# Layer 1 of a graph network: TensorE sums source rows and edge attributes by node column, with the one-hot's node numbers read from PSUM

## The chip, the cores and the metric

The kernel runs on 1 core of one Trainium2 chip. The time is device microseconds (us) of one launch. Engines are written as in the profile: PE (TensorE), DVE (VectorE), ACT (ScalarE), POOL (GpSimd), SP (SyncE, which here only issues DMAs).

## The reference, cut to what matters

There are 12,500 nodes of 128 features and 200,000 edges, sorted by target `dst`. Two layers follow each other, each with a residual and a layer norm.

```
# layer 0: attention over edges and self loops
xl, xr = x @ W_l, x @ W_r
e      = sum(leaky_relu(xl[src] + xr[dst], 0.2) * att)      # 4 heads
p      = softmax of e over the edges of a target
y      = layernorm(segment_sum(p * xl[src], dst) + bias + x) * gamma + beta
x      = layernorm(x + y)
# layer 1: message passing and a two-layer MLP
neigh  = segment_sum(x[src] + edge_attr, dst)
h      = (2 * x + neigh) @ W1 + b1
h      = where(h > 0, h, 0.01 * h)
x      = layernorm(x + h @ W2 + b2)
```

Everything is float32.

## The kernel before, in words

Edges are cut into 196 groups of 1,024 (`G`): 128 partitions by 8 edges (`T`). Nodes are padded to 100 blocks of 128. The program has five stages with a barrier of all engines between two of them (`end_phase`):

1. Linear products of all nodes. The table `xl_table` (132 columns: 128 features and 4 linear attention terms) is written to HBM.
2. Layer 0's edges: for each group POOL gathers 1,024 rows of `xl_table` by 8 indirect DMAs (line 469), PE, ACT and DVE compute the softmax and the sums.
3. Self loops, merge and the two layer norms; `x1_table` (128 columns) is written to HBM. POOL clears `xr`, which then holds `neigh`.
4. Layer 1's edges, the stage that the change rewrites.
5. The MLP and the last layer norm, over 50 pairs of blocks.

**Stage 4.** SP runs through the groups in `load_group` (line 448): once the group's ring slot is free (`rows_free1`, one of 4 slots, `U`), it loads the 1,024 source numbers (`src_idx`, line 454), then, once `dst_taken1` allows it, the targets (`dst_near`, line 458) and the attributes (512 KB into `dst_row`, line 1053). POOL waits for the source numbers and issues 8 indirect DMAs of 128 rows (`gather`, line 469). DVE, in order, for each group: subtracts the first node of the target's block from the targets (`dst_rel`, line 1105); makes a one-hot of 128 x 8 x 128 by comparing `dst_rel` with the numbers 0 to 127 in `node_row` (line 1109), both in SBUF; waits for the gather and the attributes; adds the two into `relu_h` (line 1125); frees the slot; and then adds the sum that PE made of the group before into `neigh` (line 1113). PE multiplies one-hot by message, 8 products of 128 x 128 x 128, each two instructions (line 1075). Where a group's targets lie in a second block (or more), DVE makes one more one-hot and PE sums once more (`further_visits`), and both wait for each other. One visit's one-hot therefore comes with one PE sum and one addition.

The loops over groups are `sweep`: a head, a loop of 4 groups a round, and a tail, with the ends of each group's targets loaded into registers. In stage 4 these ends are block numbers (`bounds`); in stage 2 they are the first node and the number of further windows of 128 nodes that start at that first node (`spans`).

**Stage 5.** `node_loop` interleaves steps of neighbouring pairs on each engine. For a pair: SP loads x1; DVE makes h = 2 x1 + neigh (line 1233); PE transposes it (line 1175); ACT copies it to SBUF (line 1205); PE multiplies with W1 (line 1183); ACT adds b1 (line 1210); DVE applies the slope (line 1238); PE adds residual, b2 and the product with W2 (lines 1192 to 1195); DVE takes the statistics; ACT takes the root, scales (line 885) and issues the store (line 1219).

## Time and profile before

| | |
|---|---|
| three runs | 4748.25, 4744.81, 4747.33 us; median 4747.33 |
| the profiled execution, its own time | 4730.89 us |
| its span (first to last instruction) | 4729.0 us |
| busy PE, DVE, ACT, POOL | 68%, 54%, 13%, 70% of the span |
| mean granted TensorE clock | 0.836 |
| HBM traffic | 464.45 MB read, 47.30 MB written, mean 108 GB/s |
| stages, start of each (us) | 0, 114, 2292, 2495, 4601 |

Busy shares are averages over stages with different limits, so the stage that is changed is read by itself. An instruction that only issues a DMA, waits, or works on registers is not counted as busy; an indirect DMA on POOL is, since POOL makes its descriptors.

### The profile page before, as it was taken

The numbers are of one execution on the slowest core, as the hardware profiler recorded it, in microseconds if no ns is written. First come the engines' busy times: TensorE is split into PE (matmuls) and PEld (weight loads), VectorE is DVE, ScalarE is ACT, GpSimd is POOL, SyncE is SP. The second block draws the span as 40 slices with busy tenths as digits, with TensorE's granted clock in tenths as the row PEclk, the third lists the DMA queues.
The fourth block names the chain that finished last, engine by engine and source line by source line (L and its number), as shares of the span: only waits on it lengthen the run. The fifth ranks groups of instructions, "written<-read, shape, count | busy, mean of one in ns | idle before, by whom it ended". The sixth has DMA issues, their size and how long they took to land. (4 is left out here: it accounts for less than half of the span.)

```text
span 4729.0 us, 71029 instructions
## 1 busy us (share of the span) xinstructions
PE 3216.0 (68%) x16994; PEld 2342.8 (50%) x16995; DVE 2549.1 (54%) x7518; ACT 592.0 (13%) x1636; POOL 3300.4 (70%) x3295
## 2 busy tenths in 40 slices
PE   6899999999999999999593433343333434433448
PEld 4555555565555655555483333343333333333337
DVE  7577677667666666766483333333333333333337
ACT  3111111111111111111260000000000000000006
POOL 3777777777777777776246777777777777777750
PEclk9899999999999999999796667766766676677669
DMA  6544444444444444443443333333333333333323
GB/s 183 164 111 112 112 113 112 112 112 113 113 112 113 112 112 113 112 113 99 110 114 99 103 99 95 104 100 99 104 96 102 99 100 99 99 104 99 98 71 100
DMA packets 463435, 512.49 MB, mean 108 GB/s; under 512 B 183038, under 2 KB 363134, under 8 KB 463398
## 3 DMA queue, kind: packets, MB, share of 16 engines
q1 hardware_dynamic: 280646, 262.38, 19.2%
q0 software_dynamic: 100352, 208.93, 18.0%
q10 hardware_dynamic: 82400, 40.77, 3.0%
q8 instruction: 13, 0.21, 0.0%
q14 instruction: 24, 0.20, 0.0%
HBM read 464.45 MB, written 47.30 MB: 108 GB/s over the span
## 5 line engine op out<-in xcount | busy, mean ns | idle before, releaser
L469 POOL DMA_INDIRECT rows<-xl_table,src_idx x1568 | 1587.9, 1013 | 533.6 <-issue 513.2
L469 POOL DMA_INDIRECT rows<-x_table,src_idx x1568 | 1598.6, 1020 | 489.4 <-issue 476.8
L1075 PE MATMUL pT<-relu_h,node_of 128*128 128x128 f32 x1584 | 367.8, 426 | 1017.8 <-DVE node_of L1109 1017.8
L1075 PEld LDWEIGHTS pT<-relu_h,node_of 128*128 128x128 f32 x1584 | 341.2, 327 | 1039.0 <-DVE node_of L1109 1039.0
L535 PE MATMUL ph<-node_of,xr_win 128*128 128x512 f32 x784 | 752.7, 1094 | 1.3 <-issue 1.3
L1075 PE MATMUL pA<-relu_h,edge_of 128*128 128x128 f32 x3136 | 483.7, 319 | 259.7 <-DVE relu_h L1125 259.7
L1075 PEld LDWEIGHTS pA<-relu_h,edge_of 128*128 128x128 f32 x3136 | 461.9, 234 | 278.9 <-DVE relu_h L1125 278.9
L1125 DVE TENSOR_TENSOR relu_h<-rows,dst_row 128x1024 f32<-128x1024 f32 x196 | 241.0, 1229 | 566.0 <-DMA rows<-x_table,src_idx 566.0
L572 PE MATMUL pA<-wmsg,edge_of 128*128 128x136 f32 x3168 | 425.7, 288 | 6.8 <-DVE edge_of L789 6.3
L561 PE MATMUL pT<-att_heads,relu_h 128*128 128x56 f32 x3136 | 391.3, 278 | 1.3 <-DVE shifted L818 1.3
L572 PEld LDWEIGHTS pA<-wmsg,edge_of 128*128 128x128 f32 x3168 | 385.6, 192 | 11.4 <-issue 8.0
L647 ACT ACTIVATE relu_h<-ph 128x512 f32<-128x512 f32 x392 | 234.2, 597 | 1187.7 <-PE ph L535 1177.2
L561 PEld LDWEIGHTS pT<-att_heads,relu_h 128*128 128x128 f32 x3136 | 365.9, 192 | 28.2 <-DVE shifted L818 1.4
L535 PEld LDWEIGHTS ph<-node_of,xr_win 128*128 128x128 f32 x784 | 154.1, 218 | 272.8 <-issue 272.4
L1205 ACT ACTIVATE node_of<-ph 128x256 f32<-128x256 f32 x50 | 19.2, 384 | 2146.2 <-PE ph L1175 2121.8
L1109 DVE TENSOR_TENSOR edge_of<-dst_rel,node_row 128x1024 f32<-128x1024 f32 x196 | 240.2, 1226 | 24.1
L526 PE MATMUL ph<-ident,rows 128*128 128x128 f32 x1568 | 238.2, 302 | 13.9 <-DMA rows<-xl_table,src_idx 13.9
L789 DVE TENSOR_TENSOR edge_of<-dst_rel,node_row 128x1024 f32<-128x1024 f32 x198 | 244.0, 1232 | 6.8
L1113 DVE TENSOR_TENSOR xr<-xr,pT 128x128 f32 x99 | 28.5, 288 | 400.2 <-PE pT L1075 400.2
L763 DVE TENSOR_TENSOR wmsg<-rows,wmsg 128x1024 f32<-128x1024 f32 x196 | 239.1, 1220 | 4.8 <-ACT r_exp L682 4.8
L1105 DVE TENSOR_SCALAR dst_rel<-dst_near,block_base 128x8 f32<-128x8 int32 x295 | 73.3, 248 | 270.7 <-DVE xr L1113 162.0
L526 PEld LDWEIGHTS ph<-ident,rows 128*128 128x128 f32 x1568 | 194.7, 155 | 38.4 <-issue 26.3
(154 smaller groups left out, 3637.6 us busy)
## 6 DMA issues: line engine op xcount, KB each, us to landing
dst_row<-in_dst SPq DMA_DIRECT2D x196, 513.0 KB
dst_row<-in_edge_attr SPq DMA_DIRECT2D x195, 512.0 KB
rows<-xl_table,src_idx POOLq DMA_INDIRECT x1568
rows<-x_table,src_idx POOLq DMA_INDIRECT x1568
sums_table<-win ACTq DMA_DIRECT2D x198, 68.0 KB
rows<-in_x SPq DMA_DIRECT2D x100, 128.0 KB, 2.4
xr_win<-xr_table SPq DMA_DIRECT2D x196, 64.0 KB
sums_table<-win ACTq DMA_DIRECT2D x1, 6868.0 KB
```

What stands on the lines that cost most here:

```text
L469: pool.indirect_dma_start(rows[s][:, t, 0:table.shape[1]], None, table[:, :], bass.IndirectOffsetOnAxis(ap=src_idx[s][:, t:t + 1], axis=0))\
L526: pe.matmul(h[:, t, :], rows[s][:, t, 0:D], ident[:, :], start=(t % 4 == 0), stop=False, is_transpose=True)
L535: return [pe.matmul(h[:, k:k + 4, :], xr_of[:, :], by_tile[:, k:k + 4, :], start=False, stop=stop) for k in range(0, T, 4)]
L561: pe.matmul(out_t[:, t, :], relu_h[0][:, t, :], att_heads[:, :], start=(t == 0), stop=False)
L572: ins = pe.matmul(pA[k][:, 0:WC], edge_of[k][:, t, :], w[:, t, :], start=(t == 0), stop=(t == T - 1 and k == 1))
L647: act.activation(relu_h[0][:, k:k + 4, :], h, ACT.Relu, scale=1.0 - GAT_SLOPE)\
L763: v.tensor_tensor(heads[:, :, :, 0:C], rows[s][:, :, 0:D].rearrange("p t (h c) -> p t h c", h=H), heads[:, :, :, C:HC].to_broadcast([P, T, ...
L789: one_hot = lambda k: v.tensor_tensor(edge_of[k][:, :, :], dst_rel[:, :].unsqueeze(2).to_broadcast([P, T, P]), node_row[:, :].unsqueeze(1) ...
L1075: ins = pe.matmul(banks[k][:, 0:D], edge_buf[k][:, t, :], m[:, t, :], start=(t == 0), stop=(t == T - 1))
L1105: v.tensor_scalar(dst_rel[:, :], dst_near[g.c % U][:, 1:T + 1], block_base[:, bass.ds(blk(b), 1)], None, ALU.subtract).then_inc(S("visit1_ ...
L1109: return v.tensor_tensor(edge_buf[k][:, :, :], dst_rel[:, :].unsqueeze(2).to_broadcast([P, T, P]), node_row[:, :].unsqueeze(1).to_broadcas ...
L1125: v.tensor_tensor(msg[g.c % 2][:, :, :], rows[s][:, :, 0:D], attr[s][:, :, :], ALU.add)\
```

## The change

- Stage 1 also computes `firsts`: each group's first target in every partition (a row of 196 numbers spread by a product with ones).
- Stage 4 loads all groups' targets with one DMA at its start (`dst_all`, 196 x 8 numbers in each of 128 partitions) and DVE subtracts `firsts` once (`rel_all`). The load of each group's targets falls away.
- The one-hot counts from the group's first target (as in stage 2), not from the block's first node. Its second input, the numbers 0 to 127, is in PSUM (`row_bank`).
- DVE's addition of rows and attributes falls away: PE sums both, attributes first and rows after, into one bank: 16 products in place of 8. Data are the stationary operand and the one-hot the moving one, so the sum comes out transposed: `neigh_t` has features in partitions and nodes in columns, and a window may start at any column.
- Four banks and four one-hots, one for each slot; DVE adds a bank three groups later (`LAG`). Slots are freed by PE's `neigh_summed`, not by DVE.
- Further windows are worked off by both engines before the main one of their group.
- Stage 5: PE transposes x1 itself, DVE adds `neigh_t` to twice that from PSUM and writes the transposed h, and ACT's copy falls away.

```diff
@@ sweep: head, body and tail shifted by back (LAG in stage 4)
-    part("head", None, 0, [0], 0, 2)
+    part("head", None, 0, range(back), 0, max(2, back))
     with eng.Fori(0, groups // U - 1) as j:
-        part("body", j, 0, range(1, U + 1), 0, U + 2)
+        part("body", j, 0, range(back, U + back), 0, U + max(2, back))
@@ stage 1
+                pe.wait_ge(S("first_ready"), 1)
+                pe.matmul(firsts_bank, ones[:, :], first_f[:, :], start=True, stop=True).then_inc(S("first_spread"), 1)
...
+                v.wait_ge(S("first_spread"), 1)
+                v.tensor_copy(firsts[:, :], firsts_bank)
@@ stage 4
+        banks = [t[:, 0:P] for t in (pA[0], pA[1], pT1, pT2)]
+        more_bank, row_bank = ph[0][:, 0, :], ph[1][:, 0, :]
             @block.sync
             def _(sp):
+                sp.dma_start(dst_all, bass.AP(a["dst"].tensor, 1, [[T, P], [G, groups], [1, T]])).then_inc(S("dsts_in"), 16)
+
+                def load(g, parts=P):
+                    s = g.c % U
+                    sp.wait_ge(S("neigh_summed"), g.times(1, 1))
+                    sp.dma_start(src_idx[s][:, :], bass.AP(a["src"].tensor, g.times(G), [[T, P], [1, T]]))\
+                      .then_inc(S(f"src_in1{s}"), 16)
                     src = bass.AP(a["edge_attr"].tensor, g.times(G * D), [[T * D, parts], [1, T * D]])
+                    sp.dma_start(attr[s][0:parts].rearrange("p t d -> p (t d)"), src).then_inc(S(f"attr_in{s}"), 16)
...
             @block.tensor
-                def visit(k, m):
-                    for t in range(T):
-                        ins = pe.matmul(banks[k][:, 0:D], edge_buf[k][:, t, :], m[:, t, :],
-                                        start=(t == 0), stop=(t == T - 1))
+                def visit(bank, s, one_hot):
+
+                    for k, m in enumerate((attr[s], rows[s][:, :, 0:D])):
+                        for t in range(T):
+                            ins = pe.matmul(bank, m[:, t, :], one_hot[:, t, :], start=(k == 0 and t == 0),
+                                            stop=(k == 1 and t == T - 1))
                     return ins
...
+                    wait_alone(pe, pe_waits, S(f"attr_in{s}"), g.use(16, 16))
+                    wait_alone(pe, pe_waits, S(f"gathered1{s}"), g.use(16 * T, 16 * T))
+                    further_windows(pe, n, near(g), further)
+                    pe.wait_ge(S("added"), g.times(1, 1))
+                    pe.wait_ge(S("edge_made"), g.times(1, 1))
+                    visit(banks[s], s, edge_buf[s]).then_inc(S("neigh_summed"), 1)
...
             @block.vector
+                v.tensor_copy(row_bank, node_row[:, :])
+                v.wait_ge(S("dsts_in"), 16)
+                v.tensor_tensor(rel_all, dst_all, firsts[:, :].unsqueeze(2).to_broadcast([P, groups, T]), ALU.subtract)\
...
+                def one_hot(of, rel):
+                    return v.tensor_tensor(of, rel.unsqueeze(2).to_broadcast([P, T, P]),
+                                           row_bank.unsqueeze(1).to_broadcast([P, T, P]), ALU.is_equal)
+
+                def mark(g, span):
...
+                    def further():
+                        v.reg_add(n_sum, n_sum, 1)
+                        v.reg_add(at, at, P)
+                        v.tensor_scalar(rel_more, rel_more, -float(P), None, ALU.add).then_inc(S("rel_more"), 1)
+                        v.wait_ge(S("rel_more"), count())
+                        one_hot(edge_more, rel_more).then_inc(S("again_made"), 1)
+                        v.wait_ge(S("again_summed"), count())
+                        v.tensor_tensor(nodes_from(at), nodes_from(at), more_bank, ALU.add).then_inc(S("more_added"), 1)
+                        v.wait_ge(S("more_added"), count())
+
+                    v.tensor_copy(rel_more, rel).then_inc(S("rel_copied"), 1)
+                    wait_alone(v, v_waits, S("rel_copied"), g.times(1, 1))
+                    v.reg_mov(at, span[0])
+                    further_windows(v, n, span, further)
+                    v.wait_ge(S("neigh_summed"), g.times(1, 1))
+                    one_hot(edge_buf[s], rel).then_inc(S("edge_made"), 1)
+
+                def add(g, span):
+                    v.wait_ge(S("neigh_summed"), g.times(1, U + 1))
+                    v.tensor_tensor(nodes_from(span[0]), nodes_from(span[0]), banks[g.c % U], ALU.add)\
+                     .then_inc(S("added"), 1)
...
-                        v.tensor_tensor(msg[g.c % 2][:, :, :], rows[s][:, :, 0:D], attr[s][:, :, :], ALU.add)\
-                         .then_inc(S("msg_made"), 1)
@@ stage 5
             @block.tensor
-                    pe.wait_ge(S("h_made"), q.times(1, 1))
+                    pe.wait_ge(S(f"x1_in{s2}"), q.use(16, 16, 2 * R))
...
-                        ins = pe.transpose(hT_bank[:, b * P:(b + 1) * P], h_ring[q.c % R][:, b, :], ident[:, :])
+                        ins = pe.transpose(across_bank[:, b * P:(b + 1) * P], ring_x[s2][:, b, :], ident[:, :])
             @block.scalar
-                def copy_hT(q):
-                    act.wait_ge(S("h_across"), q.times(1, 1))
-                    act.activation(hT_ring[q.c % R], hT_bank.rearrange("p (b n) -> p b n", b=2), ACT.Copy).then_inc(S("hT_ready"), 1)
             @block.vector
-                    v.scalar_tensor_tensor(h_ring[q.c % R], ring_x[s2], 2.0, neigh_pair[:, q.times(1)],
-                                           ALU.mult, ALU.add).then_inc(S("h_made"), 1)
+                    v.scalar_tensor_tensor(hT_ring[q.c % R], across_bank.rearrange("p (b n) -> p b n", b=2), 2.0,
+                                           neigh_pair[:, q.times(1)], ALU.mult, ALU.add).then_inc(S("hT_made"), 1)
```

## Rows read from the trace of the kernel before

**Rows 1.** Two stretches: from:to, length; busy us (instructions) by engine; clock, DMA share, GB/s.

```profile
3000.00:4000.00 1000.00, 391.01 (x2276) 372.46 (x2276) 360.54 (x520) 0.00 (x0) 769.36 (x758) 0.70 0.37 100
...
4620.00:4729.00 109.00, 96.22 (x526) 76.36 (x524) 75.94 (x361) 75.25 (x230) 0.00 (x0) 0.99 0.35 104
```

**Rows 2.** The page's costliest groups: count, busy us, mean ns, idle us before and what ended it.

```profile
L469 POOL DMA_INDIRECT rows<-x_table,src_idx x1568 | 1598.6, 1020 | 489.4 <-issue 476.8
...
L1113 DVE TENSOR_TENSOR xr<-xr,pT 128x128 f32 x99 | 28.5, 288 | 400.2 <-PE pT L1075 400.2
```

**Rows 3.** The instructions on the tile x_table: ns min/median/max, first and last start.

```profile
L469 POOL DMA_INDIRECT rows<-x_table,src_idx x1568: 940/945/1997, 2497.8 to 4572.9; - x196
```

**Rows 4.** Timeline of stage 4: start us, duration us, engine, line, [idle before it, what ended it].

```profile
3000.83 1.23 DVE L1109 TENSOR_TENSOR edge_of<-dst_rel,node_row 128x1024 f32<-128x1024 f32 x1
...
3001.60 1.28 POOL L469 DMA_INDIRECT rows<-x_table,src_idx  x1 [0.30 <-issue]
...
3008.18 1.26 DVE L1125 TENSOR_TENSOR relu_h<-rows,dst_row 128x1024 f32<-128x1024 f32 x1 [6.12 <-DMA rows<-x_table,src_idx]
3008.18 0.94 POOL L469 DMA_INDIRECT rows<-x_table,src_idx  x1 [0.30 <-issue]
...
3011.00 1.23 DVE L1109 TENSOR_TENSOR node_of<-dst_rel,node_row 128x1024 f32<-128x1024 f32 x1
3011.93 1.12 POOL L469 DMA_INDIRECT rows<-x_table,src_idx  x1 [0.30 <-issue]
...
3012.28 3.74 PE L1075 MATMUL pT<-relu_h,node_of 128*128 128x128 f32 x16 [11.06 <-DVE node_of L1109]
...
3015.85 1.95 PE L1075 MATMUL pA<-relu_h,edge_of 128*128 128x128 f32 x16
```

**Rows 5.** Timeline of stage 3, where POOL and DVE work side by side.

```profile
2361.07 0.73 POOL L935 TENSOR_TENSOR dst_row<-dst_row,gamma 128x256 f32<-128x256 f32 x1 [1.53 <-ACT dst_row L885]
...
2361.22 0.59 DVE L878 SCALAR_TENSOR_TENSOR stat<-stat 128x2 f32<-128x2 f32 x1
...
2364.24 0.16 DVE L878 SCALAR_TENSOR_TENSOR stat<-stat 128x2 f32<-128x2 f32 x1
2364.45 0.72 POOL L935 TENSOR_TENSOR dst_row<-dst_row,gamma 128x256 f32<-128x256 f32 x1 [2.07 <-ACT dst_row L885]
2364.56 0.49 DVE L860 BATCH_NORM_STATS2 stat<-pA 128x6 f32<-128x128 f32 x2 [0.15 <-PE pA L945]
```

**Rows 6.** The page's group of stage 2's one-hots, which count from a group's first node.

```profile
L789 DVE TENSOR_TENSOR edge_of<-dst_rel,node_row 128x1024 f32<-128x1024 f32 x198 | 244.0, 1232 | 6.8
```

**Rows 7.** Timeline of the start of stage 4.

```profile
2495.46 0.35 SPq L454 DMA_DIRECT2D src_idx<-in_src  x1
...
2497.82 0.99 POOL L469 DMA_INDIRECT rows<-x_table,src_idx  x1 [11.95 <-DMA src_idx<-in_src]
```

**Rows 8.** Stretches of 0.1 us, in which the first load of source numbers passes (columns as rows 1).

```profile
2496.40:2496.50 0.10, 0.00 (x0) 0.00 (x0) 0.00 (x0) 0.00 (x0) 0.00 (x0) 0.50 0.29 18
2496.50:2496.60 0.10, 0.00 (x0) 0.00 (x0) 0.00 (x0) 0.00 (x0) 0.00 (x0) 0.50 0.30 17
2496.60:2496.70 0.10, 0.00 (x0) 0.00 (x0) 0.00 (x0) 0.00 (x0) 0.00 (x0) 0.50 0.13 7
```

**Rows 9.** Timeline of the end of stage 4.

```profile
4576.22 1.23 DVE L1125 TENSOR_TENSOR relu_h<-rows,dst_row 128x1024 f32<-128x1024 f32 x1 [6.93 <-DMA rows<-x_table,src_idx]
...
4599.82 0.29 DVE L1113 TENSOR_TENSOR xr<-xr,pT 128x128 f32 x1 [3.91 <-PE pT L1075]
```

**Rows 10.** Timeline of stage 5: PE's transposes of two early pairs, then of two later ones.

```profile
4611.14 0.38 PE L1175 MATMUL ph<-ident,rows 128*128 128x128 f32 x2
...
4613.10 0.38 PE L1175 MATMUL ph<-ident,rows 128*128 128x128 f32 x2
...
4659.78 0.38 PE L1175 MATMUL ph<-ident,rows 128*128 128x128 f32 x2
...
4662.06 0.38 PE L1175 MATMUL ph<-ident,rows 128*128 128x128 f32 x2
```

More of the change, by code:

```diff
@@ L44 @@
 HIDE_LINKS = 1
+LAG = 3
 class Group:
@@ L81, in node_loop, with sweep @@
     steps(None, range(pairs, pairs + max(lag for _, lag in stages)))
-def sweep(eng, groups, step, ends=None, layer=0):
+def sweep(eng, groups, step, ends=None, layer=0, back=1):
     def part(tag, j, first, steps, lo, n):
@@ L94, in part @@
             step(Group(j, c), lambda g: (regs[2 * (g.c - lo)], regs[2 * (g.c - lo) + 1]))
[L96 removed]
+    part("head", None, 0, range(back), 0, max(2, back))
     with eng.Fori(0, groups // U - 1) as j:
[L98 removed]
+        part("body", j, 0, range(back, U + back), 0, U + max(2, back))
     base = groups - U
[L100 removed]
+    part("tail", None, base, range(base + back, groups + back), base, U)
 def further_windows(eng, n, span, body):
@@ L108, in further_windows @@
         eng.reg_add(n, n, 1)
-def further_visits(eng, block, ends, body):
-    first, last = ends
-    eng.reg_add(block, first, 1)
-    with eng.While(lambda: eng.snap(block) <= eng.snap(last)):
-        body()
-        eng.reg_add(block, block, 1)
 def wait_alone(eng, waits, sem, value):
@@ L181, in build @@
         ends_i = sb("ends_i", [1, 2 * groups], I32)
-        bounds = sb("bounds", [1, 2 * groups], I32)
+        firsts = sb("firsts", [P, groups])
+        first_f = sb("first_f", [1, groups])
+        ones = sb("ones", [1, P])
         spans = sb("spans", [1, 2 * groups], I32)
-        xr = sb("xr", [P, blocks, D])
+        xr = sb("xr", [P, blocks + 1, D])
         sums = sb("sums", [P, blocks, WC])
@@ L444, in _, with load_group @@
                 node_loop(v, pairs, [(hidden_self, 0), (sum_self, 2)])
+                v.wait_ge(S("first_spread"), 1)
+                v.tensor_copy(firsts[:, :], firsts_bank)
         end_phase()
[L449 removed]
+        def load_group(sp, g):
             s = g.c % U
[L453 removed]
+            sp.wait_ge(S(f"rows_free0{s}"), g.use(1, 1))
             sp.dma_start(src_idx[s][:, :], bass.AP(a["src"].tensor, g.times(G), [[T, P], [1, T]]))\
[L455 to L457 removed]
+              .then_inc(S(f"src_in0{s}"), 16)
+            sp.wait_ge(S("dst_taken0"), g.times(1, 1))
             sp.dma_start(dst_near[s][:, :], bass.AP(a["dst"].tensor, g.times(G), [[T, P], [1, T + 2]]))\
[L459 to L471 removed]
+              .then_inc(S(f"near_in0{s}"), 16)
+            sp.dma_start(dst_row[s][:, 0:G + 2], bass.AP(a["dst"].tensor, g.times(G), [[0, P], [1, G + 2]]))\
+              .then_inc(S(f"row_in0{s}"), 16)
         with nc.Block() as block:
@@ L505, in _ @@
             def _(pool):
-                gather(pool, xl_table, 0)
+                with pool.Fori(0, groups // U) as j:
+                    for s in range(U):
+                        wait_alone(pool, pool_waits, S(f"src_in0{s}"), j * 16 + 16)
+                        for t in range(T):
+                            pool.indirect_dma_start(rows[s][:, t, :], None, xl_table[:, :],
+                                                    bass.IndirectOffsetOnAxis(ap=src_idx[s][:, t:t + 1], axis=0))\
+                                .then_inc(S(f"gathered0{s}"), 16)
             @block.tensor
@@ L1065, in _ @@
             def _(pool):
-                gather(pool, x1_table, 1)
+                with pool.Fori(0, groups // U) as j:
+                    for s in range(U):
+                        wait_alone(pool, pool_waits, S(f"src_in1{s}"), j * 16 + 16)
+                        for t in range(T):
+                            pool.indirect_dma_start(rows[s][:, t, 0:D], None, x1_table[:, :],
+                                                    bass.IndirectOffsetOnAxis(ap=src_idx[s][:, t:t + 1], axis=0))\
+                                .then_inc(S(f"gathered1{s}"), 16)
@@ L1085, in further @@
                         pe.wait_ge(S("again_made"), pe.snap(n_sum, min_val=1, max_val=1 << 20))
-                        visit(2, msg[g.c % 2]).then_inc(S("again_summed"), 1)
-                    pe.wait_ge(S("msg_made"), g.times(1, 1))
-                    visit(g.c % 2, msg[g.c % 2]).then_inc(S("msg_summed"), 1)
-                    further_visits(pe, block_r, near(g), further)
-                sweep(pe, groups, step, bounds, 1)
+                        visit(more_bank, s, edge_more).then_inc(S("again_summed"), 1)
@@ L1143, in _ @@
-                sweep(v, groups, step, bounds, 1)
+                        mark(g, near(g))
+                    if g.at_least(LAG):
+                        add(g + -LAG, near(g + -LAG))
+                sweep(v, groups, step, spans, 1, LAG)
         end_phase()
         h_ring, hT_ring, out_ring = ring_a, ring_c, ring_d
-        neigh_pair = split(neigh)
+        neigh_pair = neigh_t[:, 0:nodes].rearrange("p (q b n) -> p q b n", b=2, n=P)
         flat = [t[:, :, :].rearrange("p t d -> p (t d)") for t in ph]
-        hT_bank = flat[0][:, 0:2 * P]
+        across_bank = flat[0][:, 0:2 * P]
```

112 lines of the change are left out of this document (38 added, 74 removed).

## The prediction

> **What bounds the kernel now.** I read the page's slices first. They show stages with different limits, and the change lies almost wholly in stages 4 and 5, so I asked for stretches of these alone. In stage 4 POOL is busy 769 of 1,000 us and no other engine over 391, at a DMA share of 0.37 and a mean granted TensorE clock of 0.70, so between the two levels of 1.2 and 2.4 GHz [rows 1]. POOL's idle time there is "issue", that is, nothing that it waits for: 476.8 of 489.4 us [rows 2]. 1,598.6 busy and 476.8 idle make 2,075.4 us, and the stage's gathers run from 2,497.8 to 4,572.9 plus one more instruction, 2,076.0 us [rows 3]. POOL issues without a break, so it alone sets stage 4. PE, DVE and the DMAs are beside it, and DVE waits for the gather. What the change takes from DVE is therefore worth nothing by itself. It counts only if POOL's 1,568 instructions get shorter.
>
> They can. The median one takes 945 ns, the mean 1,020 [rows 2, 3]. The timeline says when one is long: it starts while DVE is in the middle of an operation whose two inputs are both in SBUF, and it is held until that ends. L1109 runs from 3000.83 to 3002.06; POOL starts at 3001.60 with 0.46 us of it left and takes 1.28 in place of 0.94. L1109 again ends at 3012.23, POOL starts 0.30 us before and takes 1.12. The excess is the time left less 0.12 us. POOL's instruction of 3008.18, which starts with DVE's L1125 and not behind it, takes 0.94 [rows 4]. Over the stage the excess is 1,598.6 - 1,568 x 0.945 = **116.9 us**. That is all that stage 4 can give back to a faster POOL: 1,568 x 0.945 + 476.8 = 1,958.6 us is the floor, 9.99 us a group.
>
> **Stage 4, the holds.** A group has one one-hot and one message addition, and the 99 further visits have one more each [rows 2], 295 in all. After the change the message addition is gone. One-hots are 198, since windows that start at the group's first node needed just 2 further ones in stage 2, which has the same groups [rows 6]. And the one-hot's second input is in PSUM, as is one input of the addition into neigh. Does such an operation hold POOL? No row has one long enough behind which POOL starts. The bounds are the same hold as now for each one-hot, 116.9 / 295 = 0.40 us (all holds put down to the one-hots), which leaves 198 x 0.40 = 79 us, and no hold, 0 us. Stage 3 speaks for the low end. There POOL's L935 makes DVE's L878, which reads SBUF twice, last until POOL ends (0.59 us in place of 0.16), while DVE's L860, which reads PSUM, runs through POOL's next L935 unhindered, 0.49 us for two [rows 5]. I take 0: **-116.9 us**.
>
> The Trainium skill states this as a rule (SBUF — State Buffer, section "SBUF: two separate sides"): VectorE and GpSimd share one port pair as an exclusive lock, which a VectorE operation takes in a 2-port mode or with two SBUF inputs. By it the one-hot with a PSUM input takes no lock. The holds in stage 4 agree with it; no run here shows yet that a PSUM operand lifts them.
>
> **Stage 4, what hides the rest.** PE gets 16 products, 32 instructions, a group. After standing idle PE takes 3.74 us for 16 and the next 16 directly behind take 1.95 [rows 4], the ratio of the two clock levels, so a visit is 5.7 us, at worst 7.5 at the low level throughout. POOL's 9.99 us a group cover it. DVE has one one-hot of 1.23, one addition of 0.29 and a small copy; were the PSUM input read as slowly as the 128 columns in 0.288 us of L1113 [rows 2], the one-hot would be 2.3 us, still covered. Slots are freed later, by PE. From a group's last gather instruction it is 2.4 us until the rows are used [rows 3, 9], up to 7.5 for PE, 2.4 for the next source numbers [rows 7], 12.3 together, and POOL has three more groups, 30 us, to issue meanwhile. The attributes, behind the source numbers on SP's queue, have that time too. SP issues two loads a group for three. I cost all that at 0; if the cover went, each group would cost what it exceeds 9.99 by.
>
> **Stage 4, the start.** SP's first DMA is now all targets: 196 x 128 = 25,088 pieces of 32 bytes. The first source numbers are behind it on the same queue, so POOL starts later by its length. Today POOL starts 2.4 us after that load is issued [rows 7]. One load of 128 such pieces passes within 0.3 us [rows 8]: at that pace 25,088 pieces take 59 us. But it is 8 pieces for each of the 16 DMA engines, and starting and stopping make up much of it. The engines' busy time in it is (0.29 + 0.30 + 0.13) x 0.1 x 16 = 1.15 us, 9 ns a piece, and at 16 in parallel 25,088 take 14 us. A long list is nearer to the second; with some gaps between pieces I take **+28 us**, ends 14 and 59. DVE's subtraction of 1,568 columns and the first gather run side by side after it.
>
> **Stage 4, the end.** The last group has 2 further windows. Now it takes 4599.82 + 0.29 - 4576.22 = 23.9 us from its gather's arrival [rows 9], four visits of 8 products. Then it will be three of 16, each 5.7 to 7.5, with an addition, a subtraction and a one-hot (about 2.4) between them: 22 to 27 us. I take **0**, ends -2 and +4.
>
> **Stage 5.** Early pairs follow each other every 4613.10 - 4611.14 = 1.96 us, later ones every 4662.06 - 4659.78 = 2.28 [rows 10]. PE is busy in 96.2 of 109 us, ACT in 75.3 [rows 1]; from the time when ACT also issues stores, its own queue is full. Taking its copy away (0.38 us a pair) should bring the late pairs to PE's pace. About 40 pairs by 0.32 are 12.8; DVE is nearly as full and may keep some. I take **-11 us**, ends -13 and 0.
>
> **Stage 1** gets one product and one small copy from PSUM behind the last pair: **+0.5**, ends 0 and 1. Stages 2 and 3 issue the same instructions: 0.
>
> **The sum.** -116.9 + 28 + 0 - 11 + 0.5 = -99.4 us. Against the profiled execution's 4,730.9 that is 4,631.5. That execution is 16.4 us under the median of the runs, which I leave as it is: 4,747.3 - 99.4 = **4,648 us**. Ends of this case: -116.9 + 14 - 2 - 13 = -118, so 4,629; and -116.9 + 59 + 4 + 0 + 1 = -53, so 4,694; with 6 us more for small holds (the copy of 8 columns, the one subtraction with two SBUF inputs) 4,700.
>
> **Rivals.**
> - *A PSUM input does not lift the hold.* Then 79 us of holds stay and the gain is -116.9 + 79 + 28 - 11 + 0.5 = -20, 4,727 us. For it: no row of stage 4 shows the contrary. Against it: stage 3. Chance 0.07.
> - *The list of targets is slow: slower than before.* Place: SP's queue ahead of the first source numbers. Price: if the 196 parts of 128 pieces followed each other as slowly as a small load takes from issue to use, 2.36 us [rows 7], it would be 463 us, -116.9 - 10.5 + 463 = +336 in all, 5,083 us. It decides from 116.9 + 10.5 = 127 us, 5.1 ns a piece, twice the slower pace above; the pieces lie 4 KB apart in HBM where those of rows 8 are adjacent, which speaks for it, the DMA engines' short busy time against it. Chance 0.04.
> - *PE can't follow.* It needs a visit over 9.99 us where the rows give 7.5 at most; at 12 us, stage 4 would last 196 x 12 = 2,352, +276 less 11 from stage 5, 5,012 us. Chance 0.02.
>
> The Trainium skill (DMA: Bandwidth & Descriptors, section "Bandwidth") gives a floor of 0.67 us for 64 packets, about 10.5 ns each. By that the list would take 263 us and the kernel would be slower. Rows 8 show 128 pieces in 0.3 us, so this trace differs from it.
>
> **How the numbers follow.** The likeliest case has 0.87, with 4,629 to 4,700 of its own; the range goes a little below for a last visit or a start that does better, 4,624 to 4,700, and leaves out the rivals. A measurement of this kernel can tell about 0.2%, 9.5 us, from no change. Faster: 0.87 and the first rival, less a little for a mix of it with a slow list, 0.92. Within: 0.03. Slower: 0.05.
>
> **What would show it.** POOL's indirect DMAs in stage 4 with a mean near 945 ns and 0.30 between them; the first at 28 us, not 2.4, after SP's first issue; 198 one-hots; PE's visits of 32 instructions below 7.5 us; DVE or PE never the one that POOL waits for; pairs of stage 5 every 1.96 to 2.05 us. A mean that stays near 1,000 ns, or a first gather 100 us late, would make the forecast wrong.

## The result and the profile after

The changed kernel takes 4610.84 us (median of 4 runs, 4605.4 to 4611.55) against 4747.79 us (4744.81 to 4754.92), a ratio of 0.9708, 95% interval 0.9695 to 0.972. It is faster, as forecast, but by 137 us where 99 were forecast, and it ends 13 us below the range. The profiled execution took 4611.55 us (span 4609.7); that of before took 4730.89 (span 4729.0). Between these two the gain is 119.3 us.

The page of the changed kernel, costliest groups (columns as rows 2):

```profile
L1072 POOL DMA_INDIRECT rows<-x_table,src_idx x1568 | 1480.8, 944 | 504.3 <-issue 477.4
...
L1086 PE MATMUL pA<-edge_of,dst_row 128*128 128x128 f32 x1568 | 327.7, 394 | 472.3 <-DMA rows<-x_table,src_idx 389.0
```

POOL's mean is now 944 ns, where the median of before was 945 [rows 3], and 1,480.8 + 477.4 = 1,958.2 us is within 0.4 of the floor that was worked out. PE waits for POOL's rows, not POOL for PE. Two stretches of the same kernel (columns as rows 1):

```profile
3000.00:4000.00 1000.00, 554.24 (x3200) 538.11 (x3200) 172.31 (x300) 0.00 (x0) 755.94 (x802) 0.76 0.35 105
4500.00:4609.00 109.00, 101.20 (x587) 85.31 (x586) 79.71 (x395) 67.58 (x198) 0.00 (x0) 0.99 0.38 109
```

In 1,000 us of stage 4 POOL issues 802 gathers where it issued 758 [rows 1]. PE rose from 391 to 554 us and DVE fell from 361 to 172; neither matters, as neither sets the pace. Now the timeline of stage 4 in the changed kernel:

```profile
3011.16 1.22 DVE L1126 TENSOR_TENSOR edge_of<-sums,ph 128x1024 f32<-128x1024 f32 x1 [0.57 <-DVE dst_rel L1144]
3011.64 0.94 POOL L1072 DMA_INDIRECT rows<-x_table,src_idx  x1 [0.30 <-issue]
...
3012.52 3.56 PE L1086 MATMUL pA<-edge_of,dst_row 128*128 128x128 f32 x16 [2.79 <-DVE edge_of L1126]
```

POOL starts with 0.74 us of the one-hot left and takes 0.94. With both inputs in SBUF it would have taken 0.74 - 0.12 = 0.62 us longer [rows 4]. The start of the stage:

```profile
2492.66 0.38 SPq L1049 DMA_DIRECT2D sums<-in_dst  x1
...
2493.38 13.54 SPq L1054 DMA_DIRECT2D src_idx<-in_src  x1
...
2509.23 1.79 DVE L1117 TENSOR_TENSOR sums<-sums,firsts 128x1568 f32<-128x1568 int32 x1 [16.11 <-DMA sums<-in_dst]
...
2510.22 1.66 POOL L1072 DMA_INDIRECT rows<-x_table,src_idx  x1 [26.82 <-DMA src_idx<-in_src]
```

SP's second issue hangs 13.54 us behind the list, and POOL starts 17.56 us after SP's first issue where it was 2.36 [rows 7]: 15.2 us later, not 28. POOL's first instruction is the only held one of the stage: the subtraction (two inputs in SBUF) ends 0.80 us after it started, and it takes 0.71 us more than 0.944. The end of the stage:

```profile
4471.33 3.77 PE L1086 MATMUL ph<-prod,dst_row 128*128 128x128 f32 x16 [4.09 <-DMA rows<-x_table,src_idx]
...
4492.05 0.29 DVE L1153 TENSOR_TENSOR xr<-xr,pT 128x128 f32 x1 [3.07 <-PE pT L1086]
```

From the arrival of the last rows to the end of the last addition it is 4492.34 - 4471.33 = 21.0 us, against 23.9 [rows 9]. Stage 5, PE's transposes of two neighbouring pairs early and two late:

```profile
4501.63 0.38 PE L1196 MATMUL ph<-ident,rows 128*128 128x128 f32 x2
4503.59 0.38 PE L1196 MATMUL ph<-ident,rows 128*128 128x128 f32 x2
...
4550.51 0.38 PE L1196 MATMUL ph<-ident,rows 128*128 128x128 f32 x2
4552.57 0.38 PE L1196 MATMUL ph<-ident,rows 128*128 128x128 f32 x2
```

1.96 and 2.06 us, where the late ones were 2.28 apart [rows 10]. Put side by side from the two traces:

| part | forecast, us | measured between the traces, us |
|---|---|---|
| stage 4, first gather to the end of the last | -116.9 | 1958.2 - 2076.0 = -117.8 |
| stage 4, first issue of SP to the first gather | +28 | +15.2 |
| stage 4, after the last gather, with the barrier | 0 | -2.4 - 0.5 = -2.9 |
| stage 5, from SP's first load of x1 | -11 | 116.4 - 127.4 = -11.0 |
| stages 1 to 3 | +0.5 | 2492.66 - 2495.46 = -2.8 |
| sum | -99.4 | -119.3 |
| beyond the traces: the medians against the profiled executions | 0 | about -17 |

### The profile page after: what moved, and what is told of

It is laid out like the page before. It is cut to its first block and busy times, and to the rows that moved or that the text cites. A ratio compares the mean times of both kernels' runs of the same rounds, so it can differ in the third digit from the quotient of the medians.

```text
span 4609.7 us, 71384 instructions
## 1 busy us (share of the span) xinstructions
PE 3464.4 (75%) x18612; PEld 2604.3 (56%) x18613; DVE 2131.5 (46%) x7034; ACT 577.0 (13%) x1586; POOL 3181.3 (69%) x3295
## 3 DMA queue, kind: packets, MB, share of 16 engines
q0 software_dynamic: 100352, 208.93, 16.5%
## 5 line engine op out<-in xcount | busy, mean ns | idle before, releaser
L1072 POOL DMA_INDIRECT rows<-x_table,src_idx x1568 | 1480.8, 944 | 504.3 <-issue 477.4
L1086 PE MATMUL pA<-edge_of,dst_row 128*128 128x128 f32 x1568 | 327.7, 394 | 472.3 <-DMA rows<-x_table,src_idx 389.0
L1086 PE MATMUL pT<-node_of,dst_row 128*128 128x128 f32 x1568 | 324.1, 391 | 437.1 <-DMA rows<-x_table,src_idx 388.3
L1086 PEld LDWEIGHTS pA<-edge_of,dst_row 128*128 128x128 f32 x1568 | 305.9, 299 | 488.3 <-issue 486.9
L1086 PEld LDWEIGHTS pT<-node_of,dst_row 128*128 128x128 f32 x1568 | 302.4, 296 | 452.9 <-issue 451.3
L1153 DVE TENSOR_TENSOR xr<-xr,pA 128x128 f32 x98 | 28.2, 288 | 635.4 <-PE pA L1086 635.2
L782 DVE TENSOR_TENSOR edge_of<-dst_rel,node_row 128x1024 f32<-128x1024 f32 x198 | 244.1, 1233 | 6.8
L1086 PE MATMUL pT<-node_of,rows 128*128 128x128 f32 x1568 | 233.4, 313 | 0.0
L1086 PEld LDWEIGHTS pT<-node_of,rows 128*128 128x128 f32 x1568 | 231.1, 234 | 0.0
L1086 PE MATMUL pA<-edge_of,rows 128*128 128x128 f32 x1568 | 228.7, 308 | 0.0
```

The costliest lines, as they stand in the source:

```text
L782: one_hot = lambda k: v.tensor_tensor(edge_of[k][:, :, :], dst_rel[:, :].unsqueeze(2).to_broadcast([P, T, P]), node_row[:, :].unsqueeze(1) ...
L1072: pool.indirect_dma_start(rows[s][:, t, 0:D], None, x1_table[:, :], bass.IndirectOffsetOnAxis(ap=src_idx[s][:, t:t + 1], axis=0))\
L1086: ins = pe.matmul(bank, m[:, t, :], one_hot[:, t, :], start=(k == 0 and t == 0), stop=(k == 1 and t == T - 1))
L1153: v.tensor_tensor(nodes_from(span[0]), nodes_from(span[0]), banks[g.c % U], ALU.add)\
```

## The experiments

The theory was: POOL's issue alone sets stage 4; the holds go because the one-hot reads PSUM **and** the message addition is gone; the list of targets costs what it delays the first source numbers; stage 5 gains what ACT's copy cost. The rivals: one of the two alone lifts the holds; the gain comes from elsewhere (fewer visits, less work for DVE).

### Three chips on which PE's products come late

Three of the six chips that the experiments fell on ran every kernel, the kernel before too, in over 6,000 us. These runs are told first, since they change how the later ones are read. The edits are those of the next section; there the diffs stand. On the first of these chips:

> The kernel before once more, with a second profile. Its first profiled execution was 4,730.9 us, its other runs 4,744.8 to 4,754.9. Theory A: the executions of this kernel differ among themselves by some 16 us, because the holds of POOL depend on how DVE's operations fall against it; then this profile's span is near 4,745, POOL's mean in layer 1 is above 1,020 ns (16 us over 1,568 instructions are 10 ns), and the rest of the stages stays. Theory B: the difference lies in another stage, or profiled executions of this kernel are shorter than the others; then POOL's mean in layer 1 is 1,020 ns again, within 3.

> The kernel before, with only the one-hot's node numbers moved to PSUM. Theory: nearly all holds go (L1109's share), the message addition keeps some since it still reads SBUF twice; POOL's mean in layer 1 falls from 1,020 to 945-960 ns, layer 1 to some 1,960-1,985 us, and the time to about 4,640-4,660 us, so that this one edit brings over 100 of the 137 us. Rival (the holds come from the message addition as much): mean over 980 ns, 4,690 us or more.

> The kernel after, with the one-hot's node numbers read from SBUF again. Theory: an operation with two SBUF inputs holds POOL, one with a PSUM input does not. Then POOL's indirect DMAs in layer 1 get longer again, by up to 0.40 us for each of 198 one-hots, 79 us in all (mean 995 ns), and the time is 4,640 to 4,695 us. Rival (PSUM has no part in it; the message addition that DVE no longer makes, or fewer DVE instructions, ended the holds): mean within 3 ns of 944 and 4,611 us.

> The kernel after, with the load of all targets issued on ACT's queue and not ahead of the source numbers on SP's. Theory: POOL's first gather waits for nothing but its own 128 pieces behind the list; it starts 2.4 to 5 us after SP's first issue in place of 17.6, and the time falls by 10 to 15 us to 4,596-4,601 us. Rival (both queues share the DMA engines, so the source numbers still wait for the list): start 15 us or more after, time unchanged at 4,611.

Measured, against 6404.21 us for the kernel before: the kernel before again 6403.57 (1.0005, 0.9979 to 1.0031); numbers in PSUM alone 6427.95 (ratio 1.0032, 1.0004 to 1.0059); the change without PSUM numbers 6025.78 (0.9417, 0.9386 to 0.9449); the change with the list on ACT's queue 6047.69 (0.9442, 0.9412 to 0.9472). A second such chip gave the same picture, against 6412.64 us:

> The kernel before once more, since the four runs above fell on a chip where POOL also waits for source numbers (1,107 us of idle in layer 1) and every kernel takes over 6,000 us, so that they say nothing on a POOL that is the only bound. On a chip like the first: theory A (holds differ between executions) expects a span near 4,745 with POOL's mean in layer 1 at 1,025 ns or more; theory B (another stage) expects that mean at 1,020 within 3.

> The kernel before with only the node numbers moved to PSUM, on another chip. First theory: the message addition starts together with a POOL instruction or behind it as it does now, and holds stay at its 5 us; time 4,630 to 4,650. Rival, from the slow chip, where POOL's mean stayed at 999 ns with the addition as holder: the two DVE operations with two SBUF inputs replace each other, and once the one-hot no longer holds POOL the addition does; mean 985 to 1,000 ns, time 4,690 to 4,730.

> The kernel after with node numbers in SBUF, on another chip. On the slow chip POOL's mean rose from 944 to 988 ns by this edit, as the theory has it. On a chip where POOL alone bounds layer 1 that must show in the time: 69 to 79 us over the kernel after's 4,611, so 4,680 to 4,690, with a mean of 985 to 995 ns. Rival (a hold is hidden by something else): mean up, time unchanged at 4,611.

> The kernel after with the load of all targets on ACT's queue, on another chip. Theory: POOL's first gather in layer 1 starts 2.4 to 5 us after SP's first issue and not 17.6, time 4,596 to 4,601 us. Rival: the source numbers wait behind the list in the DMA engines all the same, start 15 us or more, time 4,611.

6412.27, 6423.14 (0.9995, 0.995 to 1.004), 6026.69 (0.9431, 0.9379 to 0.9484) and 6057.45 us (0.9455, 0.9407 to 0.9503). As times these were misses for every theory, because the condition that all of them shared, that POOL sets the pace, did not hold. A third such chip had the changed kernel itself (after_f, told at the end). The page's POOL group of stage 4 in the changed kernel there:

```profile
L1072 POOL DMA_INDIRECT rows<-x_table,src_idx x1568 | 1480.0, 944 | 937.5 <-issue 480.4 <-DMA src_idx<-in_src 457.2
```

The same group of the kernel before on the first of these chips:

```profile
L469 POOL DMA_INDIRECT rows<-x_table,src_idx x1568 | 1607.5, 1025 | 1106.7 <-DMA src_idx<-in_src 641.5 <-issue 465.2
```

And PE's timeline in the changed kernel on the third:

```profile
5804.19 1.95 PE L1086 MATMUL pA<-edge_of,rows 128*128 128x128 f32 x16
5805.98 1.84 PE L1086 MATMUL pT<-node_of,dst_row 128*128 128x128 f32 x15
5808.74 0.36 PE L1086 MATMUL pT<-node_of,dst_row 128*128 128x128 f32 x1 [0.93 <-issue]
...
5818.64 0.60 PE L1086 MATMUL pT<-node_of,rows 128*128 128x128 f32 x2 [1.73 <-issue]
5821.48 0.37 PE L1086 MATMUL pT<-node_of,rows 128*128 128x128 f32 x1 [2.24 <-issue]
5822.90 0.56 PE L1086 MATMUL pT<-node_of,dst_row 128*128 128x128 f32 x1 [1.05 <-issue]
```

Sixteen products pass in 1.95 us, and then single ones come with 0.9 to 2.2 us of "issue" between them, that is, with nothing that they wait for. A visit of 16 products lasts 26.4 us at worst here and 6.8 us on the chip of the case. POOL then waits 457 us for source numbers, which SP loads when PE has freed a slot. 79 of the 198 visits are longer than POOL's 9.99 us a group; on the chip of the case none is. So on these chips PE is a second bound. That its instructions reach it late is how I read "issue"; no experiment shows it. What the trace does rule out is that they are being loaded from memory meanwhile: it records the transfers of instructions too, and between 3,600 and 5,880 us of this execution there is none.

What the POOL rows say stays usable. On these chips POOL's mean in stage 4 was 1,025 and 1,017 ns in the kernel before, 999 and 992 with the numbers in PSUM alone, 988 and 994 in the change without them, and 944 in the change whole, its lists on SP's or on ACT's queue. So the holds show there as well; only the time did not follow them. Without PSUM the mean is the one that the theory had (995 ns), and with PSUM alone it is the rival's (over 980).

### Both halves, alone, on chips where POOL sets the pace

First the changed kernel once more:

> The kernel after itself, as the reference for the runs on this kind of chip. If this chip feeds PE's instructions as the first one did: 4,611 us. If it is like the two chips of the last eight runs, where PE gets its instructions one by one in about 20 us of each round of 4 groups: about 5,985 to 6,045, since the kernel after with node numbers in SBUF took 6,026 there and its holds, 69 us in all, either cost nothing while POOL waits for slots (6,026) or some 40 us (5,985).

It took 4609.29 us (4607.76 and 4610.82) against 4727.65 (4718.65 to 4728.81), ratio 0.9755, 0.9727 to 0.9783: the changed kernel is where it was, the kernel before 20 us lower. The gain is 118.4 us, about what the first two traces show (119.3). Then the three variants, on one chip, against 4720.35 us (4718.24 to 4724.11).

**The change without the numbers in PSUM:**

```diff
-        more_bank, row_bank = ph[0][:, 0, :], ph[1][:, 0, :]
+        more_bank, row_bank = ph[0][:, 0, :], node_row[:, :]
...
-                v.tensor_copy(row_bank, node_row[:, :])
```

> Again the kernel after with node numbers in SBUF, in hope of a chip where POOL alone bounds layer 1 (the kernel after took 4,609 us on the last one). Theory: POOL's mean in layer 1 rises from 944 to 985-995 ns and the time to 4,675-4,690 us. Rival (another part of the change ended the holds): mean 944, time 4,610.

4695.22 us (4688.45 to 4701.64), ratio 0.9948, 0.9932 to 0.9965. The page's POOL group:

```profile
L1072 POOL DMA_INDIRECT rows<-x_table,src_idx x1568 | 1562.5, 997 | 504.4 <-issue 477.5 <-DMA src_idx<-in_src 26.9
```

Its timeline in stage 4:

```profile
3006.32 1.23 DVE L1125 TENSOR_TENSOR node_of<-sums,node_row 128x1024 f32<-128x1024 f32 x1 [0.56 <-DVE dst_rel L1143]
3006.64 1.72 POOL L1072 DMA_INDIRECT rows<-x_table,src_idx  x1 [0.30 <-issue]
```

POOL starts 0.91 us before the one-hot's end and takes 0.78 longer. The holds are 1,562.5 - 1,568 x 0.945 = 80.7 us, close to the 79 at which the first rival priced them. The theory had a mean of 985 to 995 ns and 4,675 to 4,690 us, both a little low; its rival (944 ns, 4,610 us) is out. Without PSUM the whole rewriting is worth 25 us; the copy of 128 x 128 numbers into PSUM is worth about 85 (4695.2 against the changed kernel's 4609 to 4611, on other chips).

**The kernel before with the numbers in PSUM, and nothing else:**

```diff
+        row_bank = ph[1][:, 0, :]
...
+                v.tensor_copy(row_bank, node_row[:, :]).then_inc(S("row_copied"), 1)
+                v.wait_ge(S("row_copied"), 1)
...
-                                           node_row[:, :].unsqueeze(1).to_broadcast([P, T, P]), ALU.is_equal)
+                                           row_bank.unsqueeze(1).to_broadcast([P, T, P]), ALU.is_equal)
```

> Again the kernel before with only the node numbers in PSUM. First theory: the holds of the one-hots go, the message addition keeps its 5 us; mean 948 ns, time 4,615 to 4,640 us. Rival: the addition, two inputs in SBUF, takes the one-hot's place as holder; mean 985 to 1,000 ns, time 4,680 to 4,710 us. On the slow chips the mean was 999 ns.

4659.41 us (4658.49 to 4663.3), ratio 0.9872, 0.9855 to 0.9888. The page's POOL group:

```profile
L469 POOL DMA_INDIRECT rows<-x_table,src_idx x1568 | 1532.5, 977 | 489.6 <-issue 475.4
```

Its timeline in stage 4:

```profile
3001.40 1.22 DVE L1113 TENSOR_TENSOR edge_of<-dst_rel,ph 128x1024 f32<-128x1024 f32 x1
3001.59 0.94 POOL L469 DMA_INDIRECT rows<-x_table,src_idx  x1 [0.30 <-issue]
3002.54 1.22 DVE L1129 TENSOR_TENSOR relu_h<-rows,dst_row 128x1024 f32<-128x1024 f32 x1
3002.83 1.74 POOL L469 DMA_INDIRECT rows<-x_table,src_idx  x1 [0.30 <-issue]
```

The one-hot no longer holds POOL (0.94 at 3001.59, with 1.03 us of it left). The message addition does, and more than before: over the stage it makes 96 of POOL's instructions longer, by 52.8 us in all, where in the kernel before it was 9 and 5.1 us. (A likely reason, not tried: there the one-hot had already held POOL up until the addition was due.) The result lies between the first theory (948 ns, 4,615 to 4,640 us) and its rival (985 to 1,000 ns, 4,680 to 4,710 us), and both missed it: the addition does take over as holder, but for only about half of what the one-hots held. So each half alone leaves a good part of the holds, 81 and 51 us, and only both together leave none. Alone they are worth 25 and 61 us, together 118 (after_again), the list's cost paid.

**The change with the list of targets on ACT's queue:**

```diff
             def _(sp):
-                sp.dma_start(dst_all, bass.AP(a["dst"].tensor, 1, [[T, P], [G, groups], [1, T]])).then_inc(S("dsts_in"), 16)
...
+            @block.scalar
+            def _(act):
+                act.dma_start(dst_all, bass.AP(a["dst"].tensor, 1, [[T, P], [G, groups], [1, T]])).then_inc(S("dsts_in"), 16)
```

> Again the kernel after with the load of all targets on ACT's queue. Theory: POOL starts 2.4 to 5 us after SP's first issue in layer 1, time 4,594 to 4,599 us. Rival: it starts 15 us or more after, time 4,609 to 4,611 us.

4598.37 us (4594.59 to 4599.55), ratio 0.9739, 0.9723 to 0.9756: faster than both kernels, some 11 us below the changed one. That one ran on other chips, so the 11 us rest on its level of 4,609 to 4,611 there and on this start of stage 4, as the theory had it:

```profile
2491.67 0.40 ACTq L1066 DMA_DIRECT2D sums<-in_dst  x1
...
2491.97 0.34 SPq L1053 DMA_DIRECT2D src_idx<-in_src  x1
...
2495.30 0.99 POOL L1075 DMA_INDIRECT rows<-x_table,src_idx  x1 [12.89 <-DMA src_idx<-in_src]
...
2517.37 1.79 DVE L1120 TENSOR_TENSOR sums<-sums,firsts 128x1568 f32<-128x1568 int32 x1 [25.25 <-DMA sums<-in_dst]
```

POOL starts 3.3 us after SP's first issue, not 17.6. The list itself takes longer beside the gathers (DVE has it at 2517.4, 25.7 us after its issue), and nobody is late for that: POOL has four slots to fill, and PE and DVE catch up.

### The prices of the list and of ACT's copy, doubled or put back

Both on a further chip, against 4721.36 us (4717.8 to 4728.82). **The list of targets read twice:**

```diff
+                twin = rooms[:, 0:groups * T].bitcast(I32).rearrange("p (g t) -> p g t", t=T)
+                sp.dma_start(twin, bass.AP(a["dst"].tensor, 1, [[T, P], [G, groups], [1, T]])).then_inc(S("dsts_in"), 16)
...
-                v.wait_ge(S("dsts_in"), 16)
+                v.wait_ge(S("dsts_in"), 32)
```

> The kernel after with the list of all targets loaded twice ahead of the source numbers. Theory: a list costs what passes through the 16 DMA engines, 9 ns a piece, 25,088 pieces in 14 us; POOL starts 31 to 33 us after SP's first issue in place of 17.6, time 4,622 to 4,625 us. Rival (the price is a fixed wait at the start): POOL starts at 18 to 20 us, time unchanged at 4,610.

4626.76 us (4624.06 to 4632.3), ratio 0.9801, 0.9784 to 0.9817. The start of its stage 4:

```profile
2491.42 0.38 SPq L1050 DMA_DIRECT2D sums<-in_dst  x1
2491.86 13.84 SPq L1051 DMA_DIRECT2D sums<-in_dst  x1
2506.03 14.40 SPq L1056 DMA_DIRECT2D src_idx<-in_src  x1
```

Its first gather starts at 2523.74, 32.3 us after SP's first issue, against 17.56: the second list costs 14.8 us, nearly as much as the first (15.2), and the median is 16 us above 4610.8 (the theory had 31 to 33 us, which is met, and 4,622 to 4,625, just missed). The list's price is its length on the queue, 15 us for 25,088 pieces, 0.6 ns a piece, or 9.6 ns for one of 16 DMA engines.

**A copy of 128 x 256 put back on ACT in stage 5, for each pair:**

```diff
+                def spare(q):
+                    if q.at_least(1):
+                        act.wait_ge(S("spared"), q.times(1))
+                    act.activation(prod[:, 0:2, :], w_lr[:, 0:2 * P].rearrange("p (b n) -> p b n", b=2), ACT.Copy)\
+                       .then_inc(S("spared"), 1)
...
-                node_loop(act, pairs, [(add_b1, 1), (lambda q: root_c(act, q), 5), (finish, 7)])
+                node_loop(act, pairs, [(spare, 0), (add_b1, 1), (lambda q: root_c(act, q), 5), (finish, 7)])
```

> The kernel after with one more ACT copy of 256 columns for each pair in stage 5, in place of the one that the change removed. Theory: ACT's own queue bound the late pairs, so the pairs fall back from about 2.03 to 2.28 us, stage 5 lasts about 127 us in place of 116, time 4,620 to 4,622 us. Rival (the gain came from the shorter chain through PE and DVE): 4,610 to 4,613 us.

4623.14 us (4619.61 to 4624.91), ratio 0.979, 0.9774 to 0.9807. Its timeline, one pair late in stage 5:

```profile
4551.04 0.38 ACTq L1244 DMA_DIRECT2D out_x<-dst_row  x1
...
4551.52 0.42 ACT L1227 ACTIVATE prod<-w_lr 128x256 f32<-128x256 f32 x1 [0.65 <-ACT dst_row L878]
...
4551.85 0.46 ACT L1235 ACTIVATE rows<-pT,b 128x256 f32<-128x256 f32 x1
...
4552.20 0.29 ACT L863 ACTIVATE stat<-stat,eps 128x2 f32<-128x2 f32 x1
...
4552.39 0.80 ACT L878 ACTIVATE dst_row<-pA,stat 128x128 f32<-128x128 f32 x2
...
4553.34 0.38 ACTq L1244 DMA_DIRECT2D out_x<-dst_row  x1
```

Pairs follow every 2.30 us, which is ACT's queue: 0.38 + 0.42 + 0.46 + 0.29 + 0.80 = 2.35, with some overlap. From SP's first load of x1 to the end it is 126.0 us, against 116.4 and 116.7 in two executions of the changed kernel and 127.4 in the kernel before: about 9.5 of the 11.0 us come back with the copy. The late pairs of stage 5 were bound by ACT; what the new transposes and DVE's new operand may have brought is at most the remaining 1 to 2 us. The time is 1 us above the theory's 4,620 to 4,622, and 10 above the rival's 4,610 to 4,613.

### The level of the kernel before

The kernel before twice more, on that same chip, to see how much its own time moves:

> The kernel before, one more profile beside its time. Theory A (the spread is in POOL's holds in layer 1): this profile's span less 1,568 x (mean - 1,019.5 ns) equals 4,729 within 5 us; a span of 4,719 goes with a mean near 1,013 ns. Theory B (another stage): the mean is 1,020 within 2 and the span differs elsewhere.

> The kernel before once more, as before_d: theory A has the span follow POOL's mean in layer 1 (1,568 x mean), theory B has it not.

Medians of 4720.03 and 4722.44 us, ratios 0.9996 (0.9986 to 1.0007) and 0.9999 (0.9989 to 1.0009). POOL's group in the first:

```profile
L469 POOL DMA_INDIRECT rows<-x_table,src_idx x1568 | 1594.7, 1017 | 489.5 <-issue 477.5 <-DMA src_idx<-in_src 12.0
```

And in the second:

```profile
L469 POOL DMA_INDIRECT rows<-x_table,src_idx x1568 | 1592.4, 1016 | 489.4 <-issue 476.9 <-DMA src_idx<-in_src 12.5
```

With [rows 2] these are three executions of one kernel: spans of 4729.0, 4721.6 and 4720.2 us, holds of 116.9, 112.9 and 110.7. The holds make up 6.2 of the 8.8 us between the first and the last, and a start of stage 4 that is 2.1 us earlier most of the rest. With the difference in holds taken out, the two come to 4,725.5 and 4,726.4 us, within the 5 us of 4,729 that theory A allows, and their means of 1,017 and 1,016 ns are outside the 1,020 within 2 of theory B. The changed kernel and its variants without holds had 1,480.0 to 1,480.8 us busy in this group wherever POOL sets the pace. That its time moves with its holds is thus shown for 6 us. Whether that explains the 4,748 of the first runs, 17 us above the profiled execution, isn't: no execution of that level has a trace, the record doesn't say whether that profiled execution ran on their chip, and on three further chips of this speed none of 45 runs of that kernel was above 4728.82.

### The last two: room on PE, and a further chip

The attributes summed twice, so that a visit has 24 products (the kernel then sums rows plus twice the attributes, which is not what the reference asks), and beside it the changed kernel as it is:

```diff
-                    for k, m in enumerate((attr[s], rows[s][:, :, 0:D])):
+                    for k, m in enumerate((attr[s], attr[s], rows[s][:, :, 0:D])):
...
-                                            stop=(k == 1 and t == T - 1))
+                                            stop=(k == 2 and t == T - 1))
```

> The changed kernel with the attributes summed twice: 24 products (48 instructions) a visit in place of 16. The sum is then rows plus twice the attributes. Theory (PE has room beneath POOL's 9.99 us a group): a visit becomes 5.7 x 1.5 = 8.6 us, POOL still issues without a break, stage 4 from its first to its last gather stays within 3 us of the 1,957.5 to 1,958.2 of the changed kernel, POOL's mean stays at 944 ns, and only the last group's three visits show, 3 x 1.9 to 2.9 = 6 to 9 us more at the stage's end. Rival (PE is near to being the bound, since a visit wholly at the low clock level would take 7.5 x 1.5 = 11.3 us): stage 4 becomes up to 196 x 1.3 = 250 us longer and POOL's idle time is put down to SP's loads that wait for PE.

> The changed kernel unchanged, beside the others on this chip, to have its level and that of the kernel before on one more chip. Theory A (the level of the kernel before moves with how POOL's starts fall into DVE's operations, and only it has such holds in stage 4): this kernel is within 6 us of 4,610, whatever the kernel before reads here. Theory B (chips differ in something that both kernels have): both move together, by the same share.

Both fell on the third chip on which PE's products come late, against 6393.84 us (6362.07 to 6435.73). The changed kernel took 6059.89 us (6038.47 to 6066.3), ratio 0.947, 0.9433 to 0.9507, and with 24 products a visit 6194.25 (6188.86 to 6203.8), ratio 0.9683, 0.9647 to 0.972. The eight further products cost 134 us, between theory (at most 3 in the stage) and rival (250), but on a chip where PE is bound anyway, so the experiment does not say how much room PE has where POOL sets the pace. Theory A's figure, within 6 us of 4,610, is missed too, for the same reason, and so is theory B: against the other chips the kernel before took 1.35 times its time and the changed one 1.31, not the same share. For PE's room the trace of the changed kernel stands alone: its 198 visits last 3.8 to 6.8 us, median 5.4, under POOL's 9.99 a group.

## Why the prediction was wrong, step by step

- **What bounds the kernel: right.** POOL's issue sets stage 4, and only its held time could be had. DVE's halved and PE's half as long again busy time changed nothing.
- **The holds, -116.9: right,** -117.8. That a PSUM operand lifts the hold was taken from stage 3's small operations [rows 5]; the two variants show it by itself. The Trainium skill's rule (SBUF — State Buffer, section "SBUF: two separate sides"), that a VectorE operation takes the shared port pair when both its inputs are in SBUF, agrees with them: 944 ns with the one-hot's second input in PSUM, 997 with it in SBUF. Its other half, that a GpSimd operation which starts first makes VectorE wait, does not show for the gathers: 96 of the 99 one-hots `node_of` of stage 4 in the kernel before start in the middle of one, no later than the rest behind DVE's previous instruction (0.12 us in the median), and take 1.224 to 1.227 us like the others. The bound of 79 us for the first rival was good as well, 80.7 measured.
- **The start, +28: too large by 12.8 us.** Measured 15.2. The step that failed is "with some gaps between pieces I take +28", between ends of 14 and 59. The low end was nearly the price: 9 ns a piece through 16 engines [rows 8] against 9.6 measured, as if there were hardly any gap. That the two agree so well is in part luck, since the pieces do not pass one by one in the list. Stretches of the changed kernel in which it passes (columns as rows 1) have a DMA share above 1, so pieces of one engine overlap, and each is in flight for 14.6 ns in the mean:

```profile
2494.00:2500.00 6.00, 0.00 (x0) 0.00 (x0) 0.00 (x0) 0.00 (x0) 0.00 (x0) 0.50 1.49 64
2500.00:2506.00 6.00, 0.00 (x0) 0.00 (x0) 0.00 (x0) 0.00 (x0) 0.00 (x0) 0.50 1.87 54
```

The prediction's sign for this term, a first gather "at 28 us, not 2.4", does not fit its own sum, by which it would be 30.4; it came at 17.56. The Trainium skill (DMA: Bandwidth & Descriptors, section "Bandwidth") has a floor of about 10.5 ns a packet. The prediction multiplied it by all 25,088 pieces to get 263 us, 17 times too much. The page does not say over how many DMA engines its packets went; shared out over 16 its figure gives an estimate of 16.5 us, near the 15.2.
- **The end, 0: off by 2.9,** beyond the low end of -2 by a little: 21.0 us from the rows' arrival, where 22 to 27 were named. (From the last gather's end to the last addition it is -2.4; the barrier gives 0.5 more.) The step was "each 5.7 to 7.5", and the last three visits took 6.4, 5.4 and 3.8 us. The first, after a rest, had 3.77 and 2.80 us for its two halves, the third 2.02 and 1.95, the pace that [rows 4] show for products directly behind others.
- **Stage 5, -11: right,** -11.0, with late pairs at 2.06 where 1.96 to 2.05 were named, and by the reason given (act_copy).
- **Stages 1 to 3, +0.5:** -2.8 between the two traces. This is no gain of the change: the two further traces of the kernel before reach the first gather of stage 4 at 2494.4 and 2495.8 us, against 2497.8. The +0.5 itself is too small to be seen.
- **The level: the costliest step.** "That execution is 16.4 us under the median of the runs, which I leave as it is" put the sum on 4,747.3. This is the step that put the time below the range: with every term as measured, the median of 4,747.3 still gives 4,628.0, inside it. The terms came from an execution of 4,730.9, and the same terms on that give 4,631.5; with the measured terms 4,611.6, which is the changed kernel's time. The 37 us between 4,648 and 4,610.8 are 20 of terms (12.8 of them the list) and 17 of this. What the runs showed: the changed kernel's median (4610.84) is its profiled execution's time (4611.55), so the surplus of the kernel before did not come over. Why that kernel's first runs had it stays open. The range was built from the terms alone and had no end for that.
- **Rivals:** PSUM lifts the hold; the list is not slow; PE follows on the chips of this speed. The second rival's place was right all the same: SP's queue ahead of the source numbers was the one part that cost something, and moving it away gave a kernel that beats both.

## What to carry to other kernels

Where POOL's descriptor making sets the pace, count which DVE operations with two SBUF inputs it can run into, and take away all of them: with only the additions left, POOL fell into those instead (5 us became 53), and with only the one-hots left each still cost 0.4 us. One operand in PSUM is enough; it costs one copy, and the one-hot took 1.22 us with it for 1.23 without. A long list of small pieces goes on a queue on which nobody waits; and a forecast made from a profiled execution belongs on that execution's time, with the distance to the median as a term of its own that may vanish.

## What the runs showed of the hardware that was not expected

- One program can run at very different speeds on different chips. On three of six, single products of stage 4 came 0.9 to 2.2 us apart with nothing to wait for, and all kernels took 6,026 to 6,428 us in place of 4,598 to 4,748. The change is worth more there (0.947) than where POOL sets the pace (0.9708 and 0.9755), and the numbers in PSUM are worth nothing there (1.0032 and 0.9995 alone). What in the chips or in the program makes it so was not tried; no instructions were being loaded at the time.
- An SP queue with a list of 25,088 pieces on it holds the engine itself: the next issue took 13.5 to 14.4 us in place of 0.34.
- A held instruction of POOL is longer by what is left of DVE's operation at its start, less 0.12 to 0.13 us. One that starts ahead of DVE's operation, or up to 0.04 us behind its start, is not held; from 0.05 us on it is. This holds in the variant with 80.7 us of holds as in the kernel before. DVE's own operation suffers little: 1.22 to 1.23 us when it starts in the middle of a gather, 1.30 at most where POOL starts within 0.04 us behind it.
